# One PSUM bank moved from the ring of the maxima to the ring of the jobs, and the second product of the values cut in two

## The reference, cut to what matters

```python
h = layernorm(x) * (1 + ca) + sa                  # ca, sa, ... from silu(c) @ wmod
q, k, v = h @ Wq + bq, h @ Wk + bk, h @ Wv + bv   # 16 heads of 16 columns
attn = softmax(q k^T / 4 + 8 * position_bias)     # 512 x 512 for each head
x = x + ga * (attn @ v @ Wo + bo)
h = layernorm(x) * (1 + cb) + sb
x = x + gb * fp4_ffn(h)                           # 256 -> 704 -> 256, blocks of 16 rounded to fp4
```

## Time and profile before

| | us |
|---|---|
| median of 3 runs | 3702.15 |
| lowest and highest | 3699.88, 3706.08 |
| profiled execution | 3702.43 |
| its span, first to last instruction | 3700.5 |

### The profile page before, as it was taken

The page is one execution under the profiler, slowest core; times in us unless marked ns, Lnnn a source line. Parts: engine busy times, 40 slices in busy tenths (PEclk is TensorE's granted clock), DMA queues, the critical chain, the costliest instruction groups (busy, mean ns, idle before and its releaser), DMA issues.

```text
span 3700.5 us, 78302 instructions
## 1 busy us (share of the span) xinstructions
PE 3294.8 (89%) x20870; PEld 1927.5 (52%) x20870; DVE 2937.5 (79%) x9977; ACT 2135.1 (58%) x3352; POOL 1705.9 (46%) x2095
## 2 busy tenths in 40 slices
PE   2489999999999999999999999999999999999986
PEld 1134555555555555555555555555555555555555
DVE  7477888888888888888888888888888888888854
ACT  2256666656665666666566566666656666666552
POOL 2113444454544445454444444444445444454454
PEclk7699999999999999999999999999999999999997
DMA  3354332333223233323333432323333232333000
GB/s 99 61 98 75 60 66 52 75 76 74 62 58 65 53 74 77 74 59 61 60 58 74 77 74 53 67 56 62 74 77 74 51 68 53 65 74 71 19 21 12
DMA packets 199177, 236.76 MB, mean 64 GB/s; under 512 B 23552, under 2 KB 177568, under 8 KB 198736
## 3 DMA queue, kind: packets, MB, share of 16 engines
q1 hardware_dynamic: 198736, 231.51, 31.9%
HBM read 163.59 MB, written 67.31 MB: 62 GB/s over the span
## 4 chain that ended last, share of the span: by engine, by line
issue 48%; POOL 30%; PE 10%; DVE 5%; ACT 3%; POOLq 2%; DMA 2%; SPq 1%; ACTq 0%; DVEq 0%
POOL hidden L1270 4%; POOL hidden L1268 4%; POOL hidden L1297 4%; PE ps_x L648 4%; POOL parts L1236 3%; POOL proj L1229 3%; POOL ffn_in L1285 2%; POOL rstd L1280 2%; POOL x_mid L1263 2%; PE rings L603 1%; PE ps_o L637 1%; POOL hidden L1272 1%; POOLq L124 1%; POOL ffn_in L1301 1%; PE ps_x L674 1%
## 5 line engine op out<-in xcount | busy, mean ns | idle before, releaser
L1033 DVE CUSTOM_DVE_ANT_0 rings<-rings,band_z 128x512 f32<-128x512 f32 x2048 | 1408.4, 698 | 168.1 <-issue 165.4
L797 ACT ACTIVATE probs<-rings 128x1024 f32<-128x1024 f32 x1024 | 1049.4, 1025 | 728.3 <-PE rings L606 720.1
L619 PE MATMUL rings<-k_rows,q_rows 120*128 120x512 bf16 x2048 | 768.4, 387 | 38.1 <-DVE row_max L1033 28.7
L603 PE MATMUL rings<-q_rows,k_rows 121*128 121x512 bf16 x2048 | 728.3, 383 | 80.9 <-ACT probs L797 67.1
L637 PE MATMUL ps_o<-probs,values 128*32 128x512 f32 x4096 | 549.0, 608 | 0.9 <-ACT probs L797 0.9
L619 PEld LDWEIGHTS rings<-k_rows,q_rows 120*128 120x128 bf16 x2048 | 191.6, 97 | 519.2 <-DVE row_max L1033 285.3
L604 PE MATMUL rings<-band_t,rev 128*128 128x128 f16 x2048 | 450.8, 220 | 0.0
L606 PE MATMUL rings<-band_t,rev 128*128 128x128 f16 (+1 forms) x2048 | 431.6, 211 | 0.0
L1297 POOL TENSOR_TENSOR hidden<-hidden,inv 128x704 f32<-128x704 f32 x128 | 178.5, 1394 | 544.6 <-DVE inv L1072 544.6
L648 PE MATMUL ps_x<-w_gu_h,xq_h 128*128 128x512 f32 (+1 forms) x768 | 351.8, 458 | 20.1 <-DVE hq_l L1086 17.8
L606 PEld LDWEIGHTS rings<-band_t,rev 128*128 128x128 f16 x2048 | 201.6, 98 | 246.9 <-issue 1.8
(11 more groups left out here) (194 smaller groups left out, 6952.1 us busy)
## 6 DMA issues: line engine op xcount, KB each, us to landing
parts_dram<-parts SPq DMA_DIRECT2D x128, 384.0 KB, 2.3
q_rows<-parts_dram SPq DMA_DIRECT2D x384, 128.0 KB, 4.4
k_rows<-parts_dram SPq DMA_DIRECT2D x384, 128.0 KB, 7.1
mod_rows<-mod_rows_dram SPq DMA_DIRECT2D x32, 640.0 KB, 5.3
x_in<-in_x SPq DMA_DIRECT2D x32, 512.0 KB, 8.4
x_mid<-in_x SPq DMA_DIRECT2D x128, 128.0 KB, 2.0
out<-x_mid SPq DMA_DIRECT2D x128, 128.0 KB, 1.7
probs<-in_wmod SPq DMA_DIRECT2D x1, 1536.0 KB, 7.6
```

Of the source, the lines that this page charges most:

```text
L603: mm(ps_s[:, bank, :], kr[0:ROW_MAX + 1, h, k0:k0 + P], qr[0:ROW_MAX + 1, h, :], start=True, stop=False)
L619: mm(ps_m[:, bank, :], q_rows[par][0:ROW_MAX, h, j * P:(j + 1) * P], k_rows[par][0:ROW_MAX, h, :], start=True, stop=True).then_inc(mscores ...
L797: A(prob_pair(s, j), ps_s, ACT.Exp).then_inc(exp_done, 1)
L1033: v.tensor_tensor_reduce(ps, ps, band_z[:, bias:bias + S], 1.0, LOWEST, ALU.add, ALU.max, row_max[:, par, 4 * h + j:4 * h + j + 1]).then_i ...
```

## The change

`RING_M` goes from 3 to 2 and the ring of the jobs gets a constant of its own, `RING_X` = 3. A maxima product now waits for the reduction two before it, and a job for the reader of the job three before it. The product `v1` (four products of 128x256 results, two tiles of rows) becomes `v1` with the first of the two tiles at (2,3) and `v2` with the other at (3,3). The jobs of an iteration are then 51, a multiple of three, so that a job has the same bank in every turn of the loop. ScalarE copies `v1` and `v2` to `values` in two instructions of 256 columns, where it was one of 512. `setup_b`, used before the loop only, moves to two banks of `ps_x`.

```diff
-RING_S, RING_M = 2, 3
+RING_S, RING_M, RING_X = 2, 2, 3
...
-    batch = {(1, 1): "v0", (2, 3): "v1", (3, 2): "m1", (5, 1): "xT0", (6, 3): "xT1", (7, 2): "p0", (7, 3): "p1",
+    batch = {(1, 1): "v0", (2, 3): "v1", (3, 3): "v2", (3, 2): "m1", (5, 1): "xT0", (6, 3): "xT1", (7, 2): "p0", (7, 3): "p1",
...
-    if kind in ("v0", "v1", "m0"):
+    if kind in ("v0", "v1", "v2", "m0"):
...
-            return self.n * len(JOBS) + local, local % 2
+            return self.n * len(JOBS) + local, local % RING_X
...
-    def two_before(self, s, kind):
+    def ring_before(self, s, kind):
...
-            t, _, k = JOBS[at - 2]
-            return (self.n - 1 if at < 2 else self.n), t, k
-        past = [(m, t, k) for m in range(self.n - 2, self.n + 1) for i, (t, _, k) in enumerate(JOBS)
+            t, _, k = JOBS[at - RING_X]
+            return (self.n - 1 if at < RING_X else self.n), t, k
+        past = [(m, t, k) for m in range(self.n - 3, self.n + 1) for i, (t, _, k) in enumerate(JOBS)
...
-        setup_a, setup_b = rings[:, 0:3, :], rings[:, 3:5, :]
+        setup_a = rings[:, 0:3, :]
...
-        ps_x = ctx.enter_context(nc.psum_tensor("ps_x", [P, 2, S], F32))
+        ps_x = ctx.enter_context(nc.psum_tensor("ps_x", [P, RING_X, S], F32))
+        setup_b = ps_x[:, 1:3, :]
...
-        v_act = Steps(sem("v_act"), "v0 v1")
+        v_act = Steps(sem("v_act"), "v0 v1 v2")
...
-                    after(pe, v_act, prev, "v1")
+                    after(pe, v_act, prev, "v2")
...
-                    for k in range(2):
-                        tt = 2 * int(kind[1]) + k
+                    for k in range(2 if kind == "v0" else 1):
+                        tt = (0, 2, 3)[int(kind[1])] + k
...
-                                A(values[:, 1 - it.par, 2 * k:2 * k + 2, 0:H * VW].rearrange(
+                                A(values[:, 1 - it.par, k0:k1, 0:H * VW].rearrange(
```

More of the change, by code:

```diff
@@ L221, in job @@
             local = jobs_before(LOOP[0]) + at - LOOP[0] * len(JOBS)
-            return self.n * len(JOBS) + local, local % 2
+            return self.n * len(JOBS) + local, local % RING_X
         number = jobs_before(self.n) + sum(has_job(k, self.n, t) for t, _, k in JOBS[:at])
-        return number, number % 2
-    def two_before(self, s, kind):
+        return number, number % RING_X
+    def ring_before(self, s, kind):
         at = [(t, k) for t, _, k in JOBS].index((s, kind))
         if self.steady:
-            t, _, k = JOBS[at - 2]
-            return (self.n - 1 if at < 2 else self.n), t, k
-        past = [(m, t, k) for m in range(self.n - 2, self.n + 1) for i, (t, _, k) in enumerate(JOBS)
+            t, _, k = JOBS[at - RING_X]
+            return (self.n - 1 if at < RING_X else self.n), t, k
+        past = [(m, t, k) for m in range(self.n - 3, self.n + 1) for i, (t, _, k) in enumerate(JOBS)
                 if (m < self.n or i < at) and m >= FIRST and has_job(k, m, t)]
-        return past[-2] if len(past) > 1 else None
+        return past[-RING_X] if len(past) >= RING_X else None
 def iterations(eng, emit):
@@ L654, in job @@
                 number, bank = it.job(s, kind)
-                before = it.two_before(s, kind)
+                before = it.ring_before(s, kind)
                 if before:
@@ L853, in emit @@
                             elif kind[0] == "v":
-                                k = int(kind[1])
+                                k0, k1 = ((0, 2), (2, 3), (3, 4))[int(kind[1])]
                                 ps = read_job(it, s, kind)
-                                A(values[:, 1 - it.par, 2 * k:2 * k + 2, 0:H * VW].rearrange(
+                                A(values[:, 1 - it.par, k0:k1, 0:H * VW].rearrange(
                                     "p t (h c) -> p t h c", c=VW)[:, :, :, 1:VW],
-                                  ps.rearrange("p (t h c) -> p t h c", t=2, c=HD), ACT.Copy).then_inc(v_act.sem, 1)
+                                  ps[:, 0:(k1 - k0) * D].rearrange("p (t h c) -> p t h c", t=k1 - k0, c=HD), ACT.Copy).then_inc(v_act.sem, 1)
                             elif kind in ("m0", "m1"):
```

## The result

| | us |
|---|---|
| after, median of 4 runs | 3677.87 (3676.72 to 3680.4) |
| before, median of the 4 runs beside them | 3702.72 (3699.88 to 3706.08) |
| ratio | 0.9933, 95% interval 0.9916 to 0.9951 |
| forecast | 3681, ratio 0.9943 |

The forecast time was 3 us too high. The working behind it was less good than that: slots 6 and 10 won twice what it said, and the jump back of the loop took back the same amount, which it did not foresee. The closeness of the time is luck.

A forecast was written before the change was run, and what follows sets the result against it. TensorE's in-order stream, losing short repeated gaps, was taken as the bound. Terms 0.98 - 0.07 - 0.96 - 1.01 = -1.06 us an iteration, 0.4 given back: -0.66 x 32 = -21, from 3702.15 to 3681; 8-in-10 range 3655 to 3735.

The forecast's parts named there:

- slots 4 and 8: At (4,3) and (8,3) the maxima product waits for its bank with `wo` queued behind: 0.49 each, +0.98 us an iteration.
- slot 12: `m0` and `wo` no longer wait for job banks, but (12,3) waits for a maxima reduction: -0.07 us.
- slots 6 and 10: `xT1`, `hT1` and `p2` no longer wait for readers two jobs back: -0.96 us an iteration.
- given back elsewhere: TensorE comes nearer to 17 maxima products within 0.32 us of the new wait: +0.4 us an iteration.
- slots 15 to 3, no jump in between: Slot 15 +0.43 and slot 0 +0.49, then wins in slots 2 and 3: -0.97 us.
- slots 15 to 3 with a jump: Where the loop jumps back before slot 0: +0.83, then the wins in slots 2 and 3: -1.06 us.
- slots 15 to 3, mean: Mean over iterations with and without a jump, half of either kind: +0.88 lateness, then wins, sum -1.01 us.
- the terms for `g2`, `v1`, half of `v1` and `v2`: Slots 2 and 3: `g2` waits no more -0.66, `v1` likewise -0.42, `v1` halved -0.92, `v2` in slot 3 +0.11 us.
- +0.83, and slot 15's lateness disappears in that wait: After a jump back, (0,3) waits for its maxima bank, so slot 0's scores come 0.83 us later, absorbing slot 15's +0.43.
- The maxima ring sets the pace: Rival, slower, 28%: new maxima waits in slots 3, 7, 11 replace those of 2, 6, 10; +0.98 an iteration, 3733 us.
- The transfer moves with slot 0: Rival, no change, 16%: the `x_in` load shifts with slot 0, so `g2`'s 0.66 isn't won; 3702 us.
- Two maxima banks cost nothing: Rival, much faster, 6%: reductions come early enough and only the wins stand; -2.92 an iteration, 3609 us.

The follow-up runs named there:

- experiment 2: The kernel before with two maxima banks instead of three, the freed bank unused, two job banks, `v1` whole: 3735.08 us, ratio 1.0078.
- experiment 4: The changed kernel with `wo` put ahead of the maxima products of (0,3), (4,3) and (8,3): 3646.22 us, ratio 0.9833 to the kernel before.
- Experiments 7: The kernel before with one added TensorE wait, for the reduction of (15,1), at the end of the loop's body: 3723.77 us, ratio 1.0057.
- 5: The changed kernel with the maxima product of (15,3) issued at the head of the next iteration's slot 0: 3665.4 us, ratio 0.9899 to the kernel before.

## Why the forecast came out, and what in it was wrong

In us an iteration, mean of the two kinds, plus is later:

| step of the forecast | forecast | measured |
|---|---|---|
| slots 4 and 8 | +0.98 | +1.01 |
| slot 12 | -0.07 | -0.10 |
| slots 6 and 10 | -0.96 | -1.97 |
| given back elsewhere | +0.4 | +0.26 (slots 7, 9, 13) |
| slots 15 to 3, no jump in between | -0.97 | -1.19 |
| slots 15 to 3 with a jump | -1.06 | +1.12 |
| slots 15 to 3, mean | -1.01 | -0.04 |
| sum | -0.66 | -0.84 |

**Right, and shown.** The price of two maxima banks at (4,3), (8,3) and (0,3), 0.49 each by the forecast, is 0.46 to 0.54 in slots 4, 8 and, without a jump, 0; experiment 2 has it alone, and experiment 4 shows that it is `wo` behind the wait. Slot 15 without a jump: +0.53 where +0.43 was said. Slot 12 likewise. The transfer of `x_in` takes in the lateness of slots 15 and 0: slots 2 and 3 win 1.94 in the mean where the terms for `g2`, `v1`, half of `v1` and `v2` made 1.89. `v2` costs 0.26 or 0.06 in slot 3, 0.11 was said; its copy takes 382 ns, and slot 4 shows nothing of it beyond its own 0.5.

The Trainium skill (Perfetto Trace Analysis, Optimizing Scalar/DVE Operations) says that breaking up an instruction of ScalarE or VectorE can let work finish sooner where that engine isn't full but others stand because of it. Here ScalarE's copy was broken up together with the job of TensorE that it reads, so the runs don't test that sentence alone: the split won 14 us with a third job bank and lost 22 with two, where it met another reader's lateness. The same section says that a record in the profile shows about twice the overhead that it gives. By that the two copies would then be some 0.10 longer in the rows, an estimate, and not the 0.05 of the forecast; the rows show 0.17. The sum doesn't depend on it.

**Mis-sized: "slots 6 and 10 win 0.96".** The two gaps that the rows showed, before `xT1` and `p2`, were worth 0.43 and 0.41 (from the maxima product to them: 0.66 to 0.23, and 0.64 to 0.23), as said. The other half was in waits shorter than the tail of the record in front of them. `g2` gave 0.22 in slot 6 (the two maxima products around it were 1.51 apart, now 1.29) and 0.25 in slot 10. `hT1` gave 0.14 in slot 6 and 0.32 in slot 10 up to the scores behind it, where only 0.11 in slot 10 was counted. The first scores after `xT1` and `p2` came another 0.07 and 0.09 closer. The sum of all eight is 1.93. I had looked for gaps and brackets in the matmul rows, though the weight-load rows showed two of them and my own rule for reading a distance (a start to a start) would have shown them: 0.36 between two starts where nothing holds the second is 0.03.
The Trainium skill (Perfetto Trace Analysis, Summary: the profiler window per engine type) has a TensorE record end at an estimated time. The rows here agree: the record of 0.38 covers a start that is 0.33 later (0.36 against 0.03), of which 0.22 reached the next product.

**Wrong: after a jump "+0.83, and slot 15's lateness disappears in that wait".** Slots 15 and 0 are later by 2.79 there. The step reckoned with the waits of TensorE and not with what stands between the last of them and the first product behind the jump. Experiments 7 and 5 settle it from both sides: the younger wait alone, with no bank changed, makes +1.72, and moving the product that waits behind the jump takes the 2.21 down to 0.52. In the mean of the two kinds of iteration this is about +1.0, as much as slots 6 and 10 won beyond their term, and so the two errors cancelled. That the time came within 3 us is luck in this sense.

**Small slips of the forecast.** The product of (15,0) starts at 1978.40; 1978.38 is its weight load. Counted again, 18 of the 128 maxima products start before the end of the reduction two before, not 19, and 15 more within 0.32 of it, not 17. "Half the iterations are of either kind" is not so: 12 jumps back in 32 iterations. None of this moves its sum by more than 1 us.

**The rivals.** "The maxima ring sets the pace" asked for new waits in slots 3, 7 and 11. Over 1000 to 2800 us there are three at (3,1), of some 0.2 each, and one at (2,3); slots 7 and 11 have none that the rows show (slot 7 is 0.1 longer, why isn't shown), and slots 2, 6 and 10 kept what they won. "The transfer moves with slot 0" is out: VectorE's wait for it fell from 1.63 to 0.80, and without a jump the load is issued 9.05 behind the start of slot 0 before and 8.59 after, that is, it doesn't follow the 0.46 by which slot 0 grew. "Two maxima banks cost nothing" is out by experiment 2. The rule about repeated gaps that stood beside it (the Trainium skill, Perfetto Trace Analysis, Optimization Strategy) held for the jobs alone: with a third bank the list above has none of their gaps left (`hq_l` had 9.3 us in 12 times), and the maxima product has its own, 95.7 us in 80 times.

**Open.** Of the 3.8 to 4.7 us behind a jump, 0.9 to 1.4 is the packet of instructions, and the variation from one jump to the next goes with when that packet starts and how long it takes (correlation of their sum with the whole 0.96 to 0.98 in the four kernels). What passes in the 1.1 to 1.9 us ahead of it and in the 1.6 to 2.0 behind it, no run here shows. Nor does one show whether a smaller loop body would do without the load.

## What to carry to other kernels

When a bank moves between two rings, price each ring by distances from start to start against the reader that it will wait for, also where no gap is shown: a wait shorter than the record in front of it is real and can't be seen in the matmul rows, only in the starts and in the weight-load rows. Then look at what is queued behind each new wait, since moving that one instruction ahead (`wo` here) can be worth more than the bank (-1.0% against -0.7%). At a loop's jump, ask which wait is the last one released ahead of it, and let that one be as old as it can be.

## What the runs showed of the chip that I had not expected

A wait at the end of a loop's body that was satisfied as soon as the work around it still cost 1.72 us a turn, by moving the first product behind the jump to 3.8 to 4.5 us after its release. The amount loaded as instructions is not what differs: the kernel before and experiments 2 and 7 all have 200 packets on q8 and 241 on q14, and slot 15 before a jump lasts 7.27, 9.05 and 8.99 in them. When the load starts is: in all eleven kernels, at all 132 jumps back, a packet of q8 starts 1.1 to 2.2 us after the last wait ahead of the jump is released, takes 0.9 to 1.5, and 1.6 to 2.0 later the first product starts.
